# Reordered loads and exponentials in the scan, separate buffers for the rotation's products in attention, and an earlier weight copy: a Mamba decoder layer with mixture of experts on one core

## What is computed

```python
# 1. Mamba block: selective scan over 128 positions, 512 inner channels, 16 states
xn = layernorm(x);  x_inner, z = split(xn @ W_in);  x_conv = silu(causal_conv4(x_inner))
B, C, dt = split(x_conv @ W_x);  delta = softplus(dt);  A = -exp(A_log)
h = exp(delta*A) * h + delta * B * x_conv;   y = sum_n(h * C)       # per position
y = (y + x_conv * D_skip) * silu(z);   x1 = layernorm(x + (y @ W_out + x))
# 2. retention with rotary positions: no softmax, a decay mask instead
q, k = xpos(x1 @ W_q), xpos_inverse(ctx @ W_k);   v = ctx @ W_v
x2 = layernorm(x1 + ((q @ k.T) * decay) @ v)      # xpos: even*cos - odd*sin, odd*cos + even*sin
# 3. a shared expert and 2 of 8 routed experts
out = layernorm(x2 + shared(x2) + sum over the top 2 of w_e * down_e(silu(gate_e(x2)) * up_e(x2)))
```

## Time and profile before

| | before |
|---|---|
| time, median of 3 runs | 1773.41 us (1772.98 to 1775.08) |
| the profiled execution | 1773.41 us, of which 1771.5 us from its first to its last instruction |
| PE busy | 1677.3 us, 95% of the span |
| DVE, ACT, POOL busy | 1188.8, 803.5, 723.0 us (67%, 45%, 41%) |
| HBM traffic | 237.5 MB, 134 GB/s on the mean |
| granted clock of PE, mean | 0.977 of full speed |

### The profile page before, as it was taken

One profiled execution on the slowest core, in us unless ns is written; L12 is line 12 of the kernel. 1 busy time (PEld: TensorE's weight loads), 2 busy tenths in 40 slices (PEclk: granted clock), 3 DMA queues, 4 the chain that ended last, 5 costly groups with the idle time before them and its releaser, 6 DMA issues.

```text
span 1771.5 us, 36413 instructions
## 1 busy us (share of the span) xinstructions
PE 1677.3 (95%) x9652; PEld 1434.8 (81%) x9653; DVE 1188.8 (67%) x2735; ACT 803.5 (45%) x1507; POOL 723.0 (41%) x673
## 2 busy tenths in 40 slices
PE   6999976999998999999999987999999999999995
PEld 4777755989986888888888875888888888888884
DVE  6888866878875766766766767555555655556554
ACT  5887757778742232232232243333333333333332
POOL 1111105888961453453453443333333333333333
PEclk9999987999998999999999998999999999999998
DMA  4555564799954323323323344334445444444444
GB/s 145 186 185 184 184 232 163 225 263 267 263 209 142 103 97 117 103 95 116 102 95 116 100 163 134 56 67 92 92 91 109 92 91 94 105 90 90 105 94 105
DMA packets 155373, 237.54 MB, mean 134 GB/s; under 512 B 41824, under 2 KB 119840, under 8 KB 146992
## 3 DMA queue, kind: packets, MB, share of 16 engines
q1 hardware_dynamic: 129728, 201.29, 35.8%
q0 software_dynamic: 25584, 35.54, 11.5%
HBM read 131.11 MB, written 105.64 MB: 134 GB/s over the span
## 4 chain that ended last, share of the span: by engine, by line
PE 66%; DVE 2%; DMA 1%; issue 0%; POOL 0%; ACT 0%; SPq 0%; ACTq 0%; DVEq 0%; POOLq 0%
PE block_banks L2893 21%; PE block_banks L2913 11%; PE block_banks L2792 5%; PE block_banks L2778 5%; PE block_banks L2769 5%; PE block_banks L2695 5%; PE block_banks L2902 3%; PE block_banks L2713 2%; PE block_banks L2724 2%; PE block_banks L2732 2%; PE block_banks L2881 2%; PE block_banks L2683 1%; PE block_banks L2749 1%; DVE back_w_down L2283 1%; PE block_banks L2758 0%
## 5 line engine op out<-in xcount | busy, mean ns | idle before, releaser
L2893 PE MATMUL block_banks<-back_w_gu,back_xe_T 128*128 x1620 | 412.0, 403 | 4.8 <-DVE back_xe_T L2592 4.7
L2893 PEld LDWEIGHTS block_banks<-back_w_gu,back_xe_T 128*128 128x128 f32 x1620 | 296.7, 189 | 65.3 <-issue 5.6
L2913 PE MATMUL block_banks<-back_w_down,back_he_T 128*128 x1620 | 225.4, 288 | 1.5 <-DVE back_he_T L2604 1.5
L2913 PEld LDWEIGHTS block_banks<-back_w_down,back_he_T 128*128 128x128 f32 x1620 | 200.8, 188 | 1.8 <-issue 1.7
L1461 PE MATMUL block_banks<-front_xn_T,front_w_in_parts 128*128 128x512 f32 x768 | 189.4, 403 | 5.2 <-issue 3.3
L2063 POOL DMA_INDIRECT sorted<-back_x,back_slot x128 | 134.4, 1050 | 140.4 <-DVE back_slot L2410 92.2
L2105 POOL DMA_INDIRECT more<-back_y,back_token x67 | 103.8, 1550 | 210.9 <-DVE back_y L2611 196.6
L2105 POOL DMA_INDIRECT acc<-back_y,back_token x68 | 107.6, 1582 | 182.1 <-DVE back_y L2611 164.1
L1461 PEld LDWEIGHTS block_banks<-front_xn_T,front_w_in_parts 128*128 128x128 f32 x768 | 145.3, 193 | 42.9 <-issue 6.7
L2241 ACT ACTIVATE back_he_T<-block_banks 128x512 fp32r<-128x512 f32 x135 | 80.7, 598 | 200.0 <-PE block_banks L2902 200.0
L1276 DVE SCALAR_TENSOR_TENSOR front_conv<-block_banks,front_conv_wb,front_conv 128x508 f32<-128x508 f32 (+2 forms) x192 | 140.9, 740 | 45.1 <-ACT front_conv L1083 39.3
(11 more groups left out here) (267 smaller groups left out, 3116.9 us busy)
## 6 DMA issues: line engine op xcount, KB each, us to landing
back_xe<-sorted SPq DMA_DIRECT2D x135, 136.0 KB, 2.5
gate_T<-front_gate_T SPq DMA_DIRECT2D x16, 1024.0 KB, 4.8
xc_T<-front_xc_T SPq DMA_DIRECT2D x16, 1024.0 KB, 5.8
front_xc_in<-xc_T SPq DMA_DIRECT2D x16, 1024.0 KB, 7.8
front_gate_in<-gate_T SPq DMA_DIRECT2D x16, 1024.0 KB, 6.4
front_x_rows<-in_x SPq DMA_DIRECT2D x16, 512.0 KB, 5.6
front_c_rep<-c_parts SPq DMA_DIRECT2D x128, 64.0 KB, 5.5
front_rows_in<-in_x SPq DMA_DIRECT2D x16, 512.0 KB, 8.2
```

The source lines that it names most:

```text
L2893: op = nc.tensor.matmul(dst[:, r % 2], xe_T[:, x_part, k], w_gu[:, bass.ds(e, 1), m, w_part, k], start=(n == 0), stop=(n == len(PASSES) - 1))
L2913: op = nc.tensor.matmul(ps_y[:, 0:D_MODEL], he_T[:, h_part, k], w_down[:, bass.ds(e, 1), w_part, k], start=(n == 0), stop=(n == len(DOWN_P ...
```

## The change

Four edits, all of them to the order of work or to where it is stored; no arithmetic is different.

1. SP, scan: reps of k + 3 are issued ahead of xc of k + 2, and c of k + 3 right behind xc; x1, gate and rows follow.
2. ACT, scan: the exponential of `inner` of group k + 2 is taken at the end of step k, after `scaled` of that group, where it stood for group k + 1 behind `late` and `early` in step k.
3. DVE and POOL, attention: all four products of q and of k go into `parts`, which has four places, and POOL reads only `parts`. So the products of k wait until POOL has turned q of the same group (`xpos_ready` of 4a + 2). The wait for `scores_done` moves to POOL.
4. ACT, back: `chunk_high` stands ahead of the copy to `logits_T`, where it stood behind.

```diff
@@ SP, decoder_front, step(k, u)
+                if there(k + 1) and there(k + 3):
+                    sp.wait_ge(late_ready, k + 2)
+                    sp.wait_ge(early_ready, k + 2)
+                    load_reps(k + 3, 1 - u)
                 if there(k) and there(k + 2):
                     sp.wait_ge(skip_added, KI * (k + 1))
                     load_xc(k + 2, u)
                 if there(k + 1) and there(k + 3):
-                    sp.wait_ge(late_ready, k + 2)
-                    sp.wait_ge(early_ready, k + 2)
-                    load_reps(k + 3, 1 - u)
+                    sp.wait_ge(inner_c, k + 2)
+                    load_c(k + 3, 1 - u)
                 if there(k - 2):
                     sp.wait_ge(x1_ready, GS * (k - 1))
                     sp.dma_start(d["x1"][k - 2], x1[:, u]).then_inc(x1_stored[u], 16)
...
                     load_rows(k + 1, 1 - u)
-                if there(k + 1) and there(k + 3):
-                    sp.wait_ge(inner_c, k + 2)
-                    load_c(k + 3, 1 - u)
@@ ACT, decoder_front
-            def inner_exp_of(g):
-                act.wait_ge(scaled, g + 1)
-                nc.scalar.activation(inner, inner, ACT.Exp).then_inc(inner_exp, 1)
@@ step(k, u): behind late and early, g = k + 1
-                    if not is_at(g, 0):
-                        inner_exp_of(g)
@@ end of step(k, u)
                 if is_at(k, -2):
                     segments(0, most)
-                if is_at(k, -2):
-                    inner_exp_of(0)
+                if there(k + 2):
+                    act.wait_ge(scaled, k + 3)
+                    nc.scalar.activation(inner, inner, ACT.Exp).then_inc(inner_exp, 1)
@@ POOL, decoder_back, step
                         pool.wait_ge(parts_ready, 8 * a + 4 * which + 4)
+                        pool.wait_ge(scores_done, a)
                         for half, op in enumerate((ALU.subtract, ALU.add)):
-                            nc.gpsimd.tensor_tensor(turned_qk[:, which, half], turned_qk[:, which, half],
-                                                    parts[:, 2 * which + half], op).then_inc(xpos_ready, 1)
+                            nc.gpsimd.tensor_tensor(turned_qk[:, which, half], parts[:, 2 * half], parts[:, 2 * half + 1],
+                                                    op).then_inc(xpos_ready, 1)
@@ ACT, decoder_back, step
+                if expert and attention and u:
+                    chunk_high((g - 1) // 2)
+                if is_at(expert and g, GROUPS - 2):
+                    chunk_high(EARLY)
                 if is_at(expert and g, GROUPS - 1):
...
                     nc.scalar.activation(logits_T, ps_small[0:2 * EXPERTS], ACT.Copy).then_inc(logits_T_ready, 1)
-                if expert and attention and u:
-                    chunk_high((g - 1) // 2)
-                if is_at(expert and g, GROUPS - 2):
-                    chunk_high(EARLY)
@@ DVE, decoder_back, xpos_parts(a, which)
-                dve.wait_ge(xpos_ready, 4 * a)
-                dve.wait_ge(scores_done, a)
-                for dst, half, table in ((turned_qk[:, which, 0], 0, cos), (parts[:, 2 * which + 1], 0, sin),
-                                         (parts[:, 2 * which], 1, sin), (turned_qk[:, which, 1], 1, cos)):
+                dve.wait_ge(xpos_ready, 4 * a + 2 * which)
+                for i, half, table in ((0, 0, cos), (3, 0, sin), (1, 1, sin), (2, 1, cos)):
                     dve.wait_ge(done, 2 * a + half + 1)
-                    nc.vector.tensor_tensor(by_seq(dst), by_seq(ps_wide[:, half]), per_seq(tables[table]),
+                    nc.vector.tensor_tensor(by_seq(parts[:, i]), by_seq(ps_wide[:, half]), per_seq(tables[table]),
                                             ALU.mult).then_inc(parts_ready, 1)
```

## The result

The changed kernel takes 1797.14 us (median of 4 runs, 1794.90 to 1797.83) against 1773.20 us (4 runs, 1771.90 to 1775.08): 1.0124 times the kernel before, 95% interval 1.0108 to 1.0139. That is 24 us slower. The forecast was 1777 us, 4 us slower, with a range up to 1786. In the experiments further on one execution is left out of its row: edit 4 alone took 3423 us once, where its other eleven took 1775 to 1784.

A forecast was written before the change was run, and what follows sets the result against it. PE was taken to bound the kernel, without slack in the attention loop and nearly so in the scan. 1773.4 - 2.5 (scan) + 6.0 (attention) = 1776.9, forecast 1777 us, 8-in-10 range 1770 to 1786.

The forecast's parts named there:

- edit 2's cost: Scan: late's exponential 0.55 us later behind inner's, delaying the reps and xc; PE waits up to 0.5 us, paid half per step.
- POOL ends on time: Attention: where POOL's turning of k overlaps DVE's rounding of c, DVE waits for POOL's whole run; no cost.
- group 14's wait: Attention, group 14: POOL turns q and k in one go, later than elsewhere, so PE's up product is 1.2 us late.
- -2.5: Scan: twelve steps at 14.2 us instead of 172.94 us in all; bounds -4.3 to +16.
- rival (d): Scan: SP's cycle stays at 14.42 us, so the scan gains nothing; 1779.4 us, chance 0.10.
- rival (a): Scan: xc's load stays slow, a flight of up to 8.5 us as today; 1786 to 1795 us, chance 0.14.
- the 4.3 us to be won: Scan: twelve steps take 172.94 us against 168.6 without waits, mostly one 2.04 us wait for xc and a lower clock after it.
- the shared port: Attention: POOL's turning of k overlaps DVE's rounding of c, both inputs in SBUF; POOL was taken to end on time.
- rival (b): Attention: DVE comes between POOL's two instructions, making POOL 0.7 us late for the scores; +6.6, 1783.5 us, chance 0.12.
- Its own sign of being wrong: Attention: the prediction is wrong if the scores (L2724) wait for POOL in most steps.
- Its sum for the back: Attention loop: 6.0 us (2.8 from the rotation, 3.2 from the chunk) plus 6.6 if DVE comes between POOL's two instructions.
- Rival (c): Waits in the back cost nothing thanks to slack in PE's queue, and the scan gains all 4.3 us; 1769.6 us, chance 0.13.

The follow-up runs named there:

- edit 4 alone: The kernel before with only the chunk of high columns copied ahead of logits_T; 1.0011 times the kernel before (+2 us).
- The two controls: The kernel before and the changed kernel, each run again unaltered on other chips; 0.9998 and 1.0129 times the kernel before.
- edit 2 alone: The kernel before with only inner's exponential moved to the end of the scan step, ahead of the next late exponential; 1.0043 times the kernel before (+8 us).
- edit 1 alone: The kernel before with only SP's order changed: reps ahead of xc, c right behind it; 0.9991 times the kernel before (-2 us).
- edit 3 alone: The kernel before with only the rotation's four products put in parts and POOL waiting for scores_done; 1.0041 times the kernel before (+7 us).

## Why the prediction was wrong

Two steps of it failed: edit 2's cost, put at 0.55 us paid once in two steps where it is 1.2 us in every step, and edit 3's "POOL ends on time", where POOL ends 1 us late. The two controls give the account on undisturbed steps (1790.5 - 1767.7 = 22.8 us of span): the twelve scan steps +9.2, the steps from there to the first v projection +1.2 (one more of 15.25 us), the 14 steps between v projections +11.1, and +1.3 in the start and the end, which vary by about 2 us from one execution to the next (group 14's wait of 1.1 us, forecast as 1.2, is among them).

**Edit 2 is the step that failed.** The prediction let late's exponential be 0.55 us later, passed this on to xc, and halved it. It measured the handover from POOL to ACT correctly (416.64 to 417.7; in the changed kernel 404.78 to 405.77), but took POOL's scaling as given. It never asked what the scaling itself waits for. POOL's next scaling stands in POOL's queue behind late and early, so its own lateness comes back to it: the wait isn't 0.55 us once but makes a ring of 13.5 us of work and 1.75 us of wait. The earlier trace rows alone would have given it: the scaling ends at 416.64, POOL's late must start some 1.2 us after that (early starts at 419.14, 1.28 behind it), so it has only 1.2 us of idle time there in 14.05, and 1.75 are asked for. That gives 14.6 us a step; the rest up to 15.25 is POOL's own work grown longer (12.55 to 13.26 us), its first two gate products above all, which take 3.5 us where they take 2.5 in the kernel before. The page's 41% for POOL hid this: it is the mean over the program, and in the scan POOL is busy 89% of a step. Term: forecast inside -2.5; measured +9.2 between the controls, and edit 2 alone takes 8.6 to 9.6 us more in the twelve steps than the other three edits alone.

**Edit 1** was right in its parts (S + 10.4, 5.1 to 5.9 us, SP's cycle following PE's at 14.06, so rival (d) falls) and wrong in the sum: -2.5 forecast, -0.5 us in the scan's rows, -2 us in the runs (interval -3.7 to +0.5). The waits for xc went from one place to another and not away; rival (a)'s slow flight didn't come. That c right behind xc wouldn't slow it could not be read from the earlier trace rows, where only reps stood behind it, but edit 1 alone bears it out. And the 4.3 us to be won hung on one step of 18 us: the second profile of the kernel before has no such step, but four others of 14.4 to 16.2, and takes the same 172.8.

**Edit 3** failed at the shared port, where the prediction took the earlier trace rows (DVE waits for POOL's whole run), put the cost of the overlap at nothing and gave rival (b) 12%. Its own sign of being wrong came: with edit 3 alone L2724's scores wait for POOL in eight steps. The mechanism of (b) is what happened: DVE's rounding got in between POOL's two instructions, by 1.0 us, and moving it away takes out 0.68 us a step. Rival (b) had +0.7 in the even steps and +0.4 on top of edit 4's 0.45 in the odd ones; measured are +0.72 and +0.72 in all. Its sum for the back, 6.0 + 6.6 = 12.6 (0.7 in five steps and 0.4 in eight are 6.7), is near the 11.1 and group 14's 1.1.

The earlier trace rows was the wrong row to take, and the trace of the kernel before had a nearer one, the same two operations in group 6:

```profile
757.90 3.59 POOL L2073 TENSOR_TENSOR attention_turned_qk<-attention_turned_qk,attention_parts 128x512 f32<-128x512 f32 x2 [0.54 <-DVE attention_turned_qk L2303]
...
759.12 1.22 DVE L2294 TENSOR_TENSOR attention_c_T<-attention_c_raw,attention_c_T 128x1024 fp32r<-128x1024 f32 x1
```

POOL's two take 3.59 us here and not 2.53, as in each of the even steps but group 8's. They end at 761.49, 1.4 us ahead of the scores at 762.93, so nothing was lost. Made 2.1 us later by edit 3, they end 0.7 us behind them, and this is the cost that was measured. The rule of the Trainium skill's page "SBUF — State Buffer", an exclusive lock for the full instruction by whichever starts first, agrees with the rows of group 5 and of group 6 and not with the earlier trace rows: in group 5 DVE began 0.16 us after POOL's first instruction and ended 2.21 us later, one instruction of POOL (1.1 us left of it) and its own. The forecast's other parts held: the products of k start when POOL has turned q (735.25, which is 2.1 us later behind the v projection than before, 2.1 forecast), and group 8's up product costs 1.14 us (forecast 1.2).

**Edit 4** was right: 0.45 us at the transposes, 0.50 a step alone. But in the company of edit 3 it costs nothing. The prediction added the two; TensorE meets them one after the other in the same step, and the later one takes the earlier back. Edits 3 and 4 together: +6.0 forecast (bounds +4 to +13), +11.1 measured in these steps.

Rival (c) fell: no back step stayed at 33.23 us. Of the 23 to 24 us, then, 10.4 are edit 2's by the controls' rows (9.2 + 1.2) and some 13 by the times (1.0129 against 1.0055, each to the kernel before on its own chip, good to about 4 us), and 10.5 are edit 3's in the attention steps: 12 steps of 0.72 us and 1.85 in group 8.

## What to carry to other kernels

When an instruction of engine A is put ahead of what engine B waits for, follow B's queue on until it comes back to A's input. If it does, the cost isn't the delay of one instruction: add B's work in one step to the handover, and compare with the step. Take B's busy share from one step of that stage and not from the page, and price two waits of one engine in the same step by the later one, not by their sum. When two engines will overlap in a new way, look in the trace for the same two operations side by side before you take a row from another stage, and count how often each outcome comes.

## What was not expected of the hardware

DVE and POOL didn't share their port in one way. A DVE product of 128x1024 that starts during the first of two POOL instructions gets in between them (2.21 us instead of 1.22, POOL 3.53 instead of 2.53); in the scan two gate products are stretched alike (3.53 against 2.51). One that starts during the second waits for its end and costs POOL nothing (2.31 us at 725.89 in the kernel before). In that kernel's trace such a product starts twelve times while POOL is at one of its products with the next right behind it, and gets in between ten times. The two others are that of the earlier trace rows and that of group 8, where the rounding takes 2.96 us; in both POOL runs four instructions in a row, and DVE waits out all that are left. In the changed kernel's first profile it got in between in a run of four too, at 304.7 us. What decides this was not tried.

ACT stood for 0.6 to 0.9 us between two copies whose inputs were long ready, in even steps, which are the first of the two steps of the loop's body. All four profiles from one chip have it in four steps (groups 4, 6, 10 and 12), the changed kernel's first one has it in those and in group 2, and the kernel before's first one and the eight from the two other chips don't. On which chips the two first profiles were taken isn't on record. The trace calls the releaser remote, which names no instruction of the program. No run here tells the cause.
